# Keys shut out by the mask take the mean of the valid keys, and the row maximum becomes one fp16 number

## What is computed

```python
logits = jnp.einsum('bhqd,bhkd->bhqk', Q, K) + b[0]      # Q = layernorm(x) / sqrt(32)
logits = logits + -1e+30 * (1.0 - mask)
weights = jax.nn.softmax(logits, axis=-1)
x = x + jnp.tanh(g_xattn[0]) * einsum(weights, V)
n = layernorm(x)
x = x + jnp.tanh(g_ffn[0]) * ((silu(n @ wg.T) * (n @ wu.T)) @ wd.T)   # 256 -> 768 -> 256
```

## Time and profile before

| | |
|---|---|
| median of three runs | 167.46 us (166.77 to 167.54) |
| span of the profiled execution | 164.6 us |
| around the span, against the median | 2.9 us |
| PE busy | 142.3 us, 86% |
| DVE busy | 122.4 us, 74% |
| ACT busy | 102.8 us, 62% |
| POOL busy | 91.1 us, 55% |

### The profile page before, as it was taken

One profiled execution on the slowest core, in us unless ns is written; L12 is line 12 of the kernel. 1 busy time (PEld: TensorE's weight loads), 2 busy tenths in 40 slices (PEclk: granted clock), 3 DMA queues, 4 the chain that ended last, 5 costly groups with the idle time before them and its releaser, 6 DMA issues.

```text
span 164.6 us, 4202 instructions
## 1 busy us (share of the span) xinstructions
PE 142.3 (86%) x1459; PEld 108.3 (66%) x1459; DVE 122.4 (74%) x348; ACT 102.8 (62%) x215; POOL 91.1 (55%) x139
## 2 busy tenths in 40 slices
PE   0758779953888899999999999999999998899991
PEld 0235557642556768796879688967968766778760
DVE  4788899997099697899689968757882793874651
ACT  4236789955156677695859575957568554557540
POOL 6343450733245468468955685643576567694550
PEclk9996999987699999999999999999999999999999
DMA  3699900000000000002000100100010010010021
GB/s 111 192 358 380 301 4 0 6 0 6 10 2 0 4 0 6 0 2 68 0 0 27 45 0 2 41 27 0 4 67 1 4 52 12 0 60 10 0 68 64
DMA packets 7259, 7.95 MB, mean 48 GB/s; under 512 B 816, under 2 KB 6464, under 8 KB 7232
## 3 DMA queue, kind: packets, MB, share of 16 engines
q1 hardware_dynamic: 7056, 7.34, 13.5%
q10 hardware_dynamic: 176, 0.27, 0.5%
HBM read 5.51 MB, written 2.10 MB: 46 GB/s over the span
## 4 chain that ended last, share of the span: by engine, by line
PE 67%; DVE 18%; issue 7%; DMA 3%; ACT 1%; POOL 1%; SPq 1%; POOLq 0%; DVEq 0%; ACTq 0%
PE ps L1304 20%; PE ps L1326 10%; PE ps L1119 5%; DVE neg_max L976 5%; PE ps L1180 4%; PE ps L1236 4%; PE ps L1210 4%; PE ps L1212 4%; PE ps L1242 4%; PE ps L1183 4%; DMA gates<-in_L_xattn_b_dram 3%; PE ps L1256 3%; PE ps L1276 2%; DVE gated L1025 2%; DVE x_sb L1044 1%
## 5 line engine op out<-in xcount | busy, mean ns | idle before, releaser
L1304 PE MATMUL ps<-n_t,w_gu_t 128*128 128x256 f16 x384 | 49.9, 273 | 1.1 <-DVE h L1036 0.9
L1304 PEld LDWEIGHTS ps<-n_t,w_gu_t 128*128 128x128 f16 x384 | 36.3, 98 | 10.4 <-ACT n_t L782 2.5
L662 POOL TENSOR_TENSOR h<-h 128x256 f16<-128x256 f32 x48 | 32.2, 672 | 16.7 <-ACT h L800 16.1
L791 ACT ACTIVATE tanh_h<-ps 128x256 f32<-128x256 f32 x48 | 18.4, 384 | 17.4 <-PE ps L1304 17.3
L1326 PE MATMUL ps<-w_d_t,h 128*128 128x256 f16 x192 | 28.3, 272 | 0.8 <-DVE x_sb L1044 0.4
L976 DVE TENSOR_REDUCE neg_max<-ps 128x4 f32<-128x512 f32 x32 | 21.6, 686 | 8.9 <-PE ps L1183 8.6
L1025 DVE SCALAR_TENSOR_TENSOR gated<-tanh_h,ps 128x256 f32<-128x256 f32 x48 | 19.8, 413 | 6.6 <-ACT tanh_h L791 6.6
L744 ACT ACTIVATE probs<-ps,key_bias 128x512 f32<-128x512 f32 x32 | 22.0, 686 | 3.2 <-PE ps L1212 3.2
L616 POOL TENSOR_TENSOR rstd<-var_eps,neg_half 128x2 f32<-128x2 f32 x16 | 11.1, 696 | 22.1 <-DVE var_eps L879 22.0
L800 ACT ACTIVATE h<-h 128x256 f16<-128x256 f32 x48 | 20.0, 417 | 5.2 <-DVE h L1036 5.1
L1036 DVE SCALAR_TENSOR_TENSOR h<-ps,gated 128x256 f32<-128x256 f32 x48 | 20.4, 425 | 1.7
(11 more groups left out here) (97 smaller groups left out, 221.5 us busy)
## 6 DMA issues: line engine op xcount, KB each, us to landing
x_sb<-in_x_dram SPq DMA_DIRECT2D x8, 256.0 KB, 8.8
out_dram<-x_sb SPq DMA_DIRECT2D x8, 256.0 KB, 2.1
kv<-in_ctx_dram SPq DMA_DIRECT2D x3, 256.0 KB, 8.3
w_raw<-in_L_ffn_w_gate_dram SPq DMA_DIRECT2D x1, 768.0 KB, 7.6
w_raw<-in_L_ffn_w_up_dram SPq DMA_DIRECT2D x1, 768.0 KB, 9.3
w_raw<-in_L_ffn_w_down_dram SPq DMA_DIRECT2D x1, 768.0 KB, 8.4
kv<-in_ctx_dram ACTq DMA_DIRECT2D x1, 256.0 KB, 5.3
mask_raw<-in_mask_BxS_ik_dram ACTq DMA_DIRECT2D x1, 8.0 KB, 2.4
```

The lines of the kernel that those rows point to most:

```text
L662: pool.tensor_tensor(h16[:, r % 2, m, 1, :], h32[:, n % NHB, :], h16[:, r % 2, m, 0, :], ALU.subtract).then_inc(h_low, 1)
L1304: ins = pe.matmul(dst, lhs, rhs, start=(w == 0 and (k, l) == terms[0]), stop=(k, l) == terms[-1], skip_group_check=True)
```

## The change

The row_max steps lose the bias matmul. In its place each key that the mask shuts out is overwritten, before the keys are split and transposed, with the mean of the valid keys of its batch, so that its score is the mean of the valid scores and can't be the maximum. For this there are new steps: `k_mask` (DVE: keys times mask), `key_count` (PE: ones times the mask; DVE: a clamp, a reciprocal and two more small instructions give `fill_scale`), and `k_fill` (PE: an fp32 matmul of 256 columns sums the valid keys over the partitions; DVE: sum times `fill_scale` plus masked keys). `exp_bias` (five small DVE instructions) gives the bias of the exponential. `mask_parts` and `mask_rows` move to the wide branch. The row maximum goes as one fp16 number straight from the reduction into `max_cols16`; `max_split` stays only in the wide branch. The selector is built in fp16, and its bf16 form for the wide branch only there; POOL waits for the fp16 selector between its parts of `head_rows`. POOL also clears one more constant, `ones_full`.

```diff
-    steps = [("stats", 1, 0), ("mask_t",), ("warm_up",), ("norm1", 0), ("high", 1, 0), ("low", 1, 0), ("k_parts", 0),
-             ("mask_parts",), ("mask_rows",), ("dup", 0), ("stats", 1, 1), ("q_stack", 0, 0), ("k_stack", 0),
-             ("norm1", 1), ("q_stack", 0, 1), ("high", 1, 1), ("low", 1, 1), *maxima(0)[:3], ("dup", 1),
-             *maxima(0)[3:], sq(0), ("q_stack", 0, 2), ("max_split", 0), ("max_t", 0), ("q_stack", 0, 3),
-             ("k_parts", 1), ("stats", 1, 2)]
+    steps = [("stats", 1, 0), ("mask_t",), ("warm_up",), ("k_mask", 0), ("key_count",), ("norm1", 0), ("high", 1, 0),
+             ("low", 1, 0), ("k_fill", 0), ("k_parts", 0), ("dup", 0), ("stats", 1, 1), ("q_stack", 0, 0),
+             ("k_stack", 0), ("norm1", 1), ("q_stack", 0, 1), ("high", 1, 1), ("low", 1, 1), *maxima(0)[:2],
+             ("exp_bias",), ("dup", 1), *maxima(0)[2:], ("k_mask", 1), sq(0), ("q_stack", 0, 2), ("max_t", 0),
+             ("q_stack", 0, 3), ("k_fill", 1), ("k_parts", 1), ("stats", 1, 2)]
...
-              [("w_t", 4)], [("w_t", 5)], [], [("k_parts", 2)], [("k_stack", 2)]]
+              [("w_t", 4)], [("w_t", 5)], [("k_mask", 2)], [("k_fill", 2), ("k_parts", 2)], [("k_stack", 2)]]
...
-        put(("max_split", r + 1), when=ahead)
...
+        put(("k_mask", b + 2), when=r % 2 == 1 and r > 1 and b + 2 < B)
...
-        put(("k_parts", b + 2), when=r % 2 == 1 and r > 1 and b + 2 < B)
+        put(("k_fill", b + 2), ("k_parts", b + 2), when=r % 2 == 1 and r > 1 and b + 2 < B)
...
             for part in range(NPART):
                 if part:
-                    pool.wait_ge(pool_done, 12 + part)
+                    pool.wait_ge(pool_done, 13 + part)
+                    pool.wait_ge(selector_ready, 1)
...
+            def key_count_steps(step, plan):
+
+                dve.wait_ge(work_filled, plan.filled(step))
+                dve.tensor_scalar(counts_k[:, :], bank32(plan.bank(step))[:, 0:B], 1.0, None, ALU.max
+                                  ).then_inc(emptied_by["dve"], 1)
+                dve.wait_ge(*plan.emptied(step))
+                mine(dve.reciprocal(counts_k[:, :], counts_k[:, :]))
+                mine(dve.tensor_scalar(exp_bias[:, :], last_mask, -1.0, 1.0, ALU.mult, ALU.add))
+                wait_mine()
+                mine(dve.tensor_tensor(fill_scale[:, :], exp_bias[:, :], counts_k[:, :], ALU.mult))
+                wait_mine()
+
+            def exp_bias_steps():
+
+                dve.wait_ge(gates_loaded, 48)
+                mine(dve.tensor_scalar(exp_bias[:, :], exp_bias[:, :], MASK_STEP, gates[:, 2:3], ALU.mult, ALU.add))
+                wait_mine()
+
+                dve.tensor_scalar(exp_bias[:, :], exp_bias[:, :], gates[:, 2:3], None, ALU.subtract
+                                  ).then_inc(exp_bias_ready, 1)
+                mine(dve.tensor_scalar(checks[:, 0:B * NC], mask_k[:, :], 0.0, None, ALU.not_equal))
+                mine(dve.tensor_scalar(checks[:, NZERO:NZERO + B], last_mask, 1.0, None, ALU.is_ge))
+                wait_mine()
+
+                mine(dve.scalar_tensor_tensor(
+                    out=checks[:, 0:B * NC].rearrange("p (b c) -> p b c", c=NC)[:, :, LAST], in0=last_mask, scalar=0.0,
+                    in1=last_mask, op0=ALU.not_equal, op1=ALU.not_equal))
...
+                    elif kind == "k_mask":
 
                         b = step[1]
                         dve.wait_ge(kv_loaded[b], 16)
+                        dve.tensor_scalar(k_valid[:, b % 2, :], kv[:, b, 0:D], last_mask[:, b:b + 1], None, ALU.mult
+                                          ).then_inc(keys_masked, 1)
+                    elif kind == "k_fill":
...
+                        dve.wait_ge(work_filled, plan.filled(step))
...
+                        dve.scalar_tensor_tensor(out=k_filled[:, b % 2, :], in0=bank32(plan.bank(step))[:, 0:D],
+                                                 scalar=fill_scale[:, b:b + 1], in1=k_valid[:, b % 2, :],
+                                                 op0=ALU.mult, op1=ALU.add).then_inc(emptied_by["dve"], 1)
...
+                    elif kind == "key_count":
+                        n = open_work(plan, step)
+                        pe.wait_ge(*plan.emptied(("mask_t",)))
+                        pe.matmul(bank32(n)[:, 0:B], ones_full[:, :], last_mask, start=True, stop=True
+                                  ).then_inc(work_filled, 1)
+                    elif kind == "k_fill":
+                        b = step[1]
+                        n = open_work(plan, step)
+                        pe.wait_ge(keys_masked, b + 1)
+                        pe.matmul(bank32(n)[:, 0:D], ones_full[:, :], k_valid[:, b % 2, :], start=True, stop=True
+                                  ).then_inc(work_filled, 1)
...
-                                pe.matmul(bank32(n)[:, j * P:(j + 1) * P], q_stacks[:, b, h, qt * P:(qt + 1) * P],
-                                          k_stacks[:, b, h, :], start=(j == 0), stop=False, skip_group_check=True)
-                        rows = bias_rows[:, b * NC + c, :].unsqueeze(1).to_broadcast((P, HG, P))
-                        pe.matmul(bank32(n), ones_b[:, :], rows, start=False, stop=True, skip_group_check=True
-                                  ).then_inc(work_filled, 1)
+                                ins = pe.matmul(bank32(n)[:, j * P:(j + 1) * P],
+                                                q_stacks[:, b, h, qt * P:(qt + 1) * P], k_stacks[:, b, h, :],
+                                                start=(j == 0), stop=True, skip_group_check=True)
+                        ins.then_inc(work_filled, 1)
```

More of the change, by code:

```diff
@@ L113, in emptied_by_engine @@
 def emptied_by_engine(kind, step):
-    if kind in ("mask_t", "k_stack", "flag_sum", "row_max", "attn_t", "k_block"):
+    if kind in ("mask_t", "key_count", "k_fill", "k_stack", "flag_sum", "row_max", "attn_t", "k_block"):
         return "dve"
@@ L272, in wide_steps @@
     drain = [("weigh_o", 0, 1, 1, c), ("weigh_d", 0, 1, 0, c), ("weigh_d", 0, 1, 1, c), ("o_copy", 0, 1, 1)]
-    steps = []
+    steps = [("mask_parts",)]
     for b in range(B):
@@ L697, in run @@
                             act.activation(tanh_g[:, :], gates[:, 0:2], ACT.Tanh).then_inc(tanh_ready, 1)
+                    elif kind == "mask_parts":
+                        act.wait_ge(pool_done, CONSTS)
+                        act.activation(max_sel[:, :, :], head_rows[:, :].unsqueeze(2).to_broadcast((P, NH, P)),
+                                       ACT.Copy).then_inc(selector_ready, 1)
                     elif kind == "mask_rows":
@@ L734, in run @@
                         act.wait_ge(work_filled, plan.filled(step))
-                        act.activation(max_rows[:, n % 2, :], bankb(plan.bank(step))[:, 0:SH],
-                                       ACT.Copy).then_inc(emptied_by["act"], 1)
+                        if is_wide:
+                            act.activation(max_rows[:, n % 2, :], bankb(plan.bank(step))[:, 0:SH],
+                                           ACT.Copy).then_inc(emptied_by["act"], 1)
+                        else:
+                            act.activation(max_rows16[:, n % 2, :], bank16(plan.bank(step))[:, 0:SH],
+                                           ACT.Copy).then_inc(emptied_by["act"], 1)
                     elif kind == "scores":
@@ L1174, in run @@
                                       skip_group_check=True)
+                            rows = bias_rows[:, b * NC + c, :].unsqueeze(1).to_broadcast((P, HG, P))
+                            ins = pe.matmul(bank32(n), ones_b[:, :], rows, start=False, stop=True,
+                                            skip_group_check=True)
                         else:
```

108 lines of the change are left out of this document (66 added, 42 removed).

## The result

The changed kernel takes 170.92 us (median of 5 runs), the kernel before 166.77 us beside it: the ratio is 1.0275 [1.0206, 1.0343], slower by 4.15 us. The forecast was slower by 2.15. The time itself lies in the range of 166.5 to 171.2, but the change is about twice as large as forecast.

The account below looks back on a forecast made before the run. Bounds: a chain of short steps at the start, DVE from 20 to 40 us, PE in rounds 3 to 6. Terms 3.3 + 2.2 - 1.6 + 1.2 - 2.95 = +2.15 gave span 166.75, plus 2.9: 169.6 us; range 166.5 to 171.2.

Parts of the forecast that it names:

- A: Start to first row_max matmul: DVE waits behind the warm-up, POOL holds dup, transposes run at low clock; +3.3 us.
- B: First row_max matmul to the next head group's first reduction: added exp_bias, k_mask(1), k_fill(1) outweigh removed work; +2.2 us.
- C: Rounds 0 and 1 up to the branch: DVE-bound, two max_splits leave; -1.6 us, bounds -2.0 and -1.2.
- the branch: From the last DVE instruction ahead of the branch to the first behind it: forecast change 0.
- D: Round 2, after the branch: k_mask(2) and k_fill(2) delay PE and the keys; +1.2 us, bounds 0 and 1.65.
- E: Rounds 3 to 6, PE-bound: 16 bias matmuls go (3.4 us), k_fill(3) adds 0.45; net -2.95 us.
- k_mask(2) longer than 1 us: Sign expected in round 2: k_mask(2), with a POOL instruction in its way, takes more than 1 us.
- PE's gain wins: Rival: rounds 3 to 6's -2.95 decides if delay up to the branch is below about 2 us; 166.1 us, chance 0.16.
- the two cancel: Rival: smaller delays at the start and in round 2 offset the later gain; +0.25, 167.7 us, chance 0.20.
- The clock rival: Rival: PE's clock is low in other parts of the DVE-bound stage, losing up to 1 us; 171.5 us, chance 0.10.
- The wide branch: Rival: the check, with limit 16000 instead of 60000, takes the wide branch; far above 171.5 us, chance 0.01.

Follow-up runs that it names:

- warm_after_fill: Changed kernel with the eight warm-up matmuls moved behind key_count and the first k_fill; 168.06 us, ratio 1.0072.
- dup_first: Changed kernel with dup(0) ahead of k_parts(0) in the list; 174.32 us, one execution.
- before_fp16_max: Kernel before with the maximum as one fp16 number and no max_split in the narrow part, bias matmul kept; 164.52 us, ratio 0.9844.
- before_both: Kernel before without the bias matmul and with the fp16 maximum, without key count and key fill; 161.54 us, ratio 0.9706.
- late_fill: Changed kernel with warm-up behind the first key fill, second fill in round 0's chores, exp_bias behind stats(1, 2), k_mask(2) in round 2's first chore; 164.49 us.
- late_fill_warm_first: As late_fill, but with the warm-up back at its place of the changed kernel, ahead of key_count; 169.84 us, ratio 1.0159.
- after_again: The changed kernel once more, unaltered, for a second profile; 170.58 us, span 168.8 us.

## Why the prediction was off

**The time itself is near in part by luck.** The 169.6 us were put on 2.9 us "around the span", but that is the span of one execution set against the median of others: in nearly every execution on record the time is 1.8 to 2.0 us above its own span. With the forecast change of 2.15 on 166.77 us the forecast time would have been 168.9, 2 us short.

**A was right, a little short.** norm1(0) was forecast at 9.7 and came at 9.82, `dup` is held by POOL to 13.84 (13.75), and the first row_max matmul is at 16.66 (16.4); 3.6 is just above the bound of 3.4. `warm_after_fill` and `dup_first` show that both mechanisms are what they were taken for.

**B was right in its sum, wrong in a term.** 2.5 against 2.2. `exp_bias`'s L867 was held as said (0.98 us), but the round trip of `k_fill(1)`, put at 0.9 us of idle DVE, with half of 1.1 more for a low clock, is 2.11: the fp32 product alone takes 1.16 us at the low clock.

**C is the step that failed.** "Two max_splits leave it: -1.6" reads a busy DVE as a sum of durations. That holds where no key fill stands in front: C is -1.5 in `before_fp16_max` and -1.6 in `before_both`. In the changed kernel the work did fall, by 1.2 us of busy time, and C came out at +1.1, 2.7 off. The other misses (A +0.3, B +0.3, the branch -1.0, D -0.5, E +0.25) add up to -0.65, so that C is more than the whole error of 2.05 by the spans. The prediction let the second key fill end at the reduction in B and never followed what is queued behind it: `stats(1, 2)`, which begins the chain of group 2 (power and norm on POOL, `high` on ACT with the exponential behind it). From DVE's reduction of the variance to `dup` this chain takes some 4.7 us in both kernels (19.71 to 24.43 before). Before, it began before the reductions, which with `max_split` filled it; after, it begins with them at 26.34, the norm collides with the weight cast (1.78 instead of 1.09), and DVE and PE run dry: 1.16 idle for DVE before `dup`, 3.91 for PE before L1321. After that PE's clock is 0.63 from 30 to 33.5 us, which holds further DVE copies back (L1018 waits 0.94 for PE). So C gave +1.1 where -1.6 was forecast. Against `before_both` 1.4 of the 2.7 us lie between the reduction and `dup` (4.67 us for 3.27), and 1.2 between `dup` and the check (11.3 for 10.0), where `before_both` has PE at full clock and after has it at 0.85. `late_fill` and `late_fill_warm_first` show that the place of the second fill is the cause of the delay up to the check. That the 1.2 us are the low clock's, and how much the cast has of the 1.4, is argued and not shown.

**The branch**, put at nothing, was 1.0 shorter: DVE's 4.94 us of idle time before its first instruction behind it became 3.96, now put down to PE. It is the lighter maxima's: `before_both` has 3.82 there. Why they shorten it stays open.

**D** was +0.7 instead of 1.2, within its bounds, but only where round 2 has the full clock: in the other execution of the changed kernel it was +4.2 (18.7 us for 14.5), and the prediction had no term for the clock there. Its step "k_mask(2) longer than 1 us" held in that execution (1.28) and was wrong in this one (timeline of after):

```profile
51.16 0.56 DVE L1018 COPY w_d_t<-ps 128x768 f16<-128x768 f16 x1 [3.96 <-PE ps L1258]
...
54.66 0.35 DVE L957 TENSOR_SCALAR k_valid<-kv,mask_k 128x256 f32<-128x256 f32 x1
```

**E was right**: -2.7 against -2.95, round by round 0.4, 0.8, 0.8 and 0.7 us. Its two terms hold as well: -3.2 in `before_both` (3.4 forecast), and `k_fill(3)` with what belongs to it adds 0.5 to that (0.45 forecast). With the bias matmuls alone taken out it is -2.8, and with `max_split` alone nothing (62.4 us in `before_fp16_max`), so some of the gain needs both gone.

**The rivals.** That PE's gain wins needed a delay of under 2 us up to the branch; it was 7.2. That the two cancel needed A 2.8 and B 1.5; they were 3.6 and 2.5. The clock rival named something that is there (0.63 from 30 to 33.5 us), but as a loss of its own; here it comes right behind PE's 3.91 us of idle time, so it is taken for a result of the fill's place, which is argued. That its 171.5 is near the time is partly chance. Ahead of the reduction a lower clock cost nothing, as the two executions of the changed kernel show. The wide branch was not taken.

**Open.** The effects of the two moves don't add: the warm-up's place is worth 2.5 us beside the early second fill and 5.3 beside the late one (medians 170.58 to 168.06, 169.84 to 164.49). The traces put it in round 2: without the warm-up ahead of the key count that round is 1.1 us longer in one pair (16.3 for 15.2) and 1.5 shorter in the other (16.1 for 17.7), and its length goes with the clock granted there. But no run set the clock on its own.

## What to carry to other kernels

A step that waits for a round trip to another engine costs more than its own wait: write down which chains start behind it in the in-order list, and whether they still start before the work that used to cover them. Filler work for PE belongs behind every small product that another engine waits for. When instructions leave an engine that is busy all the time, ask which chain they were filling before counting them as won. And take two executions' traces of one kernel before reading a difference of a microsecond or two from one stage: here the same kernel took 15.2 and 18.7 us for the same round.

## What was not expected of the hardware

- A DVE instruction of four elements per partition (L867) took 0.98 us beside a POOL instruction of 1.15 us (timeline of after):

```profile
18.30 1.15 POOL L657 TENSOR_TENSOR q_parts<-norm,q_parts 128x512 f16<-128x512 f32 x1 [2.54 <-ACT q_parts L706]
18.49 0.98 DVE L867 TENSOR_SCALAR exp_bias<-exp_bias,gates 128x4 f32<-128x4 f32 x1
```

- It works the other way too: two norm instructions of POOL take 1.78 us where a weight cast of DVE lies beside them, and 1.09 or 1.10 where they begin ahead of it.
- The fp32 product of 256 columns took 0.97 us before round 0 and 0.49 at full clock in round 3 (the chain that ended last, of after):

```profile
22.99 0.97 PE ps L1178 x2
...
79.44 0.49 PE ps L1178 x2
```

- The warm-up matmuls of 512 columns start 0.43 us apart, twice the 0.21 of such a matmul in rounds 3 to 6 of before, though the clock row of the profile's page shows 9 there. The distance of starts is the better witness of the clock than the digit. The Trainium skill, page "TensorE: Matmul & The Clock Gate", section "Wait — 56ns, not 53.3ns?", gives 426.7 ns for 512 columns while the array is cold; the trace agrees.
- A kernel whose start is 3.4 us shorter ends 4.7 us sooner, and another one, 3.7 us shorter, 2.9 sooner; what the first wins on the way (1.5 us) and the second loses (1.1) comes in round 2.
- A low clock cost nothing in one stretch and microseconds in another. The same kernel in two executions, the other one and then `after_again`, with the reduction that ends B at 26.08 and 26.18 us:

```profile
13.00:26.60 13.60, 10.71 (x80) 8.90 (x81) 10.29 (x29) 6.88 (x12) 3.82 (x5) 0.50 0.54 187
```

```profile
13.00:26.60 13.60, 9.69 (x88) 8.09 (x88) 10.29 (x29) 6.88 (x12) 3.82 (x5) 0.75 0.55 191
```

PE is busier and DVE does the same. In round 2 the same two executions differ by 3.4 us, at 0.83 and 0.99.
